# Sixteen of 98 target tiles of a graph propagation step summed from gathered feature rows instead of a dense product

## The reference

```python
def step(f, _):
    f = f * src_norm[:, None]
    agg = jax.ops.segment_sum(f[src], dst, num_segments=n)   # n = 12500 nodes, 200000 edges
    f = agg * dst_norm[:, None]
    f = (1.0 - ALPHA) * f + ALPHA * feat0
    return (f, None)
feat, _ = jax.lax.scan(step, feat, None, length=K)           # K = 10
x = x + feat
```

## Time and profile before

| | |
|---|---|
| median of three runs | 6389.11 us |
| span of the profiled execution | 7018.8 us |
| TensorE busy with matmuls in it | 5576.3 us (79%) |
| VectorE busy | 4279.1 us (61%) |
| GpSimd busy | 1693.3 us (24%) |
| mean granted TensorE clock | 0.880 |
| propagation: first to last sweep matmul | 3003 to 6987 us of the span |

### The profile page before, as it was taken

How to read it: one execution, slowest core, us unless ns; L and a number is a source line. 1 busy time by engine, 2 the same in 40 slices (tenths; PEclk the granted TensorE clock), 3 DMA queues, 4 the chain that set the end, 5 groups by cost and what they waited for, 6 DMA issues and landing times. The chain is left out here.

```text
span 7018.8 us, 211605 instructions
## 1 busy us (share of the span) xinstructions
PE 5576.3 (79%) x85008; PEld 3590.0 (51%) x85008; DVE 4279.1 (61%) x12668; ACT 721.3 (10%) x1695; POOL 1693.3 (24%) x1739
## 2 busy tenths in 40 slices
PE   1455555555555556589999999999999999999998
PEld 1344444444444445446565554656555565656564
DVE  7455555555555557766666666666656666666665
ACT  0122222222222223000000000000000000000000
POOL 5655555555555552500000000000000000000000
PEclk9867676666667767799999999999999999999999
DMA  4322222222222222155545555555555555555554
GB/s 117 77 75 76 76 76 77 75 76 77 79 72 79 72 76 94 27 205 194 200 183 204 192 198 205 189 200 191 201 191 201 191 201 201 189 203 189 197 197 169
DMA packets 442864, 1016.61 MB, mean 145 GB/s; under 512 B 253162, under 2 KB 371914, under 8 KB 387354
## 3 DMA queue, kind: packets, MB, share of 16 engines
q1 hardware_dynamic: 386938, 968.76, 39.0%
q0 software_dynamic: 54944, 33.96, 2.6%
HBM read 838.78 MB, written 176.58 MB: 145 GB/s over the span
## 5 line engine op out<-in xcount | busy, mean ns | idle before, releaser
L1864 PE MATMUL banks_fast<-count_units_fast,feature_parts_fast 128*32 128x512 fp8e3 x70608 | 3826.3, 379 | 31.6 <-DVE count_units_fast L1759 26.9
L1864 PEld LDWEIGHTS banks_fast<-count_units_fast,feature_parts_fast 128*32 128x32 bf16 x70608 | 2146.2, 97 | 1688.5 <-issue 37.5
L1758 DVE TENSOR_SCALAR count_units_fast<-packed_ring_fast 128x512 int32<-128x512 int32 x2949 | 1255.8, 426 | 1429.1 <-PE banks_fast L1864 1398.2
L144 POOL DMA_INDIRECT rows_fast<-row_table,idx_fast x1456 | 1408.5, 967 | 996.9 <-ACT count_stage_fast L1257 563.4
L1759 DVE TENSOR_SCALAR count_units_fast<-packed_ring_fast 128x512 int32<-128x512 int32 x2949 | 1237.2, 420 | 0.0
L1351 PE MATMUL banks_fast<-w1a_b1a_fast,turn_fast 49*128 49x96 f32 x3136 | 374.6, 375 | 810.6 <-ACT turn_fast L1262 589.6
L1223 DVE TENSOR_SCALAR window_place_hot_fast<-iota_wide_fast,local_keys_fast,target_weight_fast 128x196 bf16<-128x196 f16 x3136 | 933.9, 343 | 0.0
L1316 PE MATMUL banks_fast<-window_place_hot_fast,window_src_hot_fast 128*128 128x196 bf16 x3136 | 697.4, 312 | 115.4 <-issue 71.0
L1322 PE MATMUL banks_fast<-window_place_hot_fast,window_src_hot_fast 128*128 128x196 bf16 x3136 | 680.2, 305 | 106.1 <-issue 105.4
L1351 PEld LDWEIGHTS banks_fast<-w1a_b1a_fast,turn_fast 49*128 49x128 f32 x3136 | 294.9, 260 | 917.4 <-issue 497.4
L1316 PEld LDWEIGHTS banks_fast<-window_place_hot_fast,window_src_hot_fast 128*128 128x128 bf16 x3136 | 410.1, 155 | 224.2 <-issue 148.3
(11 more groups left out here) (282 smaller groups left out, 1551.5 us busy)
## 6 DMA issues: line engine op xcount, KB each, us to landing
packed_ring_fast<-edge_counts SPq DMA_DIRECT2D x422, 1792.0 KB, 7.0
edge_counts<-count_stage_fast SPq DMA_DIRECT2D x100, 784.0 KB
running_sums<-run_sums_fast SPq DMA_DIRECT2D x100, 768.0 KB
rows_fast<-row_table,idx_fast POOLq DMA_INDIRECT x1456
rows_fast<-attrs_padded SPq DMA_DIRECT2D x98, 128.0 KB
attrs_padded<-in_edge_attr SPq DMA_DIRECT2D x1, 12500.0 KB
rows_fast<-row_table,src_ends_fast POOLq DMA_INDIRECT x112
row_table<-h_nodes_fast SPq DMA_DIRECT2D x1, 1568.0 KB, 5.2
```

The source lines that it names most:

```text
L144: pool.indirect_dma_start(out=self.rows[:, r, c, 0:DN], out_offset=None, in_=b.dram.table, in_offset=bass.IndirectOffsetOnAxis(ap=idx[:, c ...
L1758: nc.vector.tensor_scalar(to[..., 0:P // 8], of, NIBBLES, None, ALU.bitwise_and)
L1864: last = nc.tensor.matmul(b.banks[at:at + DN, SWEEP[m % 2], 0:COLS], parts[:, side, j, k * DN:(k + 1) * DN], of_strip.bitcast(FP8), start= ...
```

## The change

The six blocks become five. The last sixteen target tiles (82 to 97) get no dense product. Since edges are sorted by target, the last 32,768 edges hold all edges of these tiles. They are cut into 256 gathers of 128 edges. For each, GpSimd gathers with an indirect DMA the 192-byte feature rows of the 128 source nodes from a table in DRAM (`feature_rows`, one for odd and one for even steps), and TensorE multiplies them with a one-hot matrix (`gathered_hots`, made once) of 128 edges by 128 targets: 96 weight columns, up to 128 moving columns. The 128 targets are a window that moves by 8 from gather to gather. The sums of four tiles fill a PSUM bank, and two banks are used in turn; a window that crosses from one bank to the next takes two matmuls, which makes 301 matmuls a step, and four zero matmuls of 512 columns clear the banks.

The table is written from the parts by DMAs on ScalarE's queue, ten a step: one behind each block's features, the head's and the four banks'. GpSimd begins a step's gathers when all ten of the step before have landed, and may be 32 gathers ahead of TensorE (eight slots of four). TensorE takes eight gathers at a time, a visit, between two sweep units; the units are given by a formula (unit 23, then one visit each 7.3 units, 32 visits, the last after unit 243 of 245). Banks are folded six units after their last visit, the fourth beside the fifth block's fold. VectorE has four more sets of features, of four tiles each. `x` is saved to DRAM and its tile holds the gathered rows; it comes back in the last step. Ahead of the loop, once: the edges' ends are loaded and turned, and VectorE makes the one-hots in eight instructions of 4096 columns. If an edge lies outside its window, the flag for the general way is set.

```diff
-BLOCKS = J // TILES
+BLOCKS = J // TILES - 1
+FIRST_GATHERED = HEAD + BLOCKS * TILES
+GATHERS = 256
+BANK_TILES = 4
+GROUP = 4
+GSLOTS = 8
+PE_GROUPS = 2
+PER_TARGET = E // N
+def window_of(c):
+    centre = (N - P * FIRST_GATHERED) - ((GATHERS - c) * P - P // 2) // PER_TARGET
+    return min(max(centre - P // 2, 0), TILES * P - P)
...
+        visit_unit = lambda visit: (230 + 73 * visit - (54 if visit >= 18 else 0)) // 10
+        fold_unit = [visit_unit(v) + FOLD_BEHIND for v in bank_visit[:-1]]
+        feature_unit = [u + LEAD for u in fold_unit]
...
         def _(pool):
+            with pool.Fori(0, steps2) as tt:
+                for side in range(2):
+                    t = tt * 2 + side
+                    pool.wait_ge(table_stored[side], tt * (STORES * 16) + (STORES * 16 if side else 16))
+                    for g in range(STEP_GROUPS):
+                        pool.wait_ge(group_used, t * STEP_GROUPS + (g + 1))
+                        for i in range(GROUP):
+                            c = g * GROUP + i
+                            pool.indirect_dma_start(out=rows[:, g % GSLOTS, i, :], out_offset=None, in_=b.dram.feature_rows[side],
+                                                    in_offset=bass.IndirectOffsetOnAxis(ap=idx[:, c:c + 1], axis=0)).then_inc(rows_in[g % GSLOTS], 16)
...
         def _(act):
+            def keep_block(t, side, m):
+                act.wait_ge(fresh, t * BLOCKS + (m + BLOCKS + 1))
+                keep_rows(1 - side, slice(HEAD + m * TILES, HEAD + (m + 1) * TILES))
...
+                    drain_bank(t, 3)
+                    drain_block(t, side, 4)
+                    keep_bank(t, side, 3)
+                    keep_block(t, side, 4)
...
         def _(dve):
+            for c in range(0, GATHERS, PIECE):
+                nc.vector.tensor_tensor(hots[:, c:c + PIECE, :], b.iota16[:, :].unsqueeze(1).broadcast_to([P, PIECE, P]),
+                                        local16[:, c:c + PIECE].unsqueeze(2).broadcast_to([P, PIECE, P]), ALU.is_equal).then_inc(hots_made, 1)
...
+                        if m == BLOCKS - 1:
+                            bank_features(t, q, side, GBANKS - 1)
+                        block_features(t, q, side, m)
...
         def _(pe):
+            def gathered_sums(t, visit):
+                for g in range(visit * PE_GROUPS, (visit + 1) * PE_GROUPS):
+                    pe.wait_ge(rows_in[g % GSLOTS], t * (STEP_GROUPS // GSLOTS * GROUP * 16) + (g // GSLOTS + 1) * (GROUP * 16))
+                    for i in range(GROUP):
+                        c = g * GROUP + i
...
+                        for lo, hi in ((w, cut), (cut, w + P)):
+                            if lo < hi:
+                                last = nc.tensor.matmul(b.banks[0:WF, GATHER_BANK[k % 2], lo - k * BANK_COLS:hi - k * BANK_COLS],
+                                                        rows[:, g % GSLOTS, i, :], hots[:, c, lo - w:hi - w].bitcast(FP8),
+                                                        start=False, stop=False, skip_group_check=True)
+                    last.then_inc(group_used, 1)
...
+            def sweep_and_gather(t, m, side, first, last_unit):
+                for v in range(first, last_unit):
+                    sweep_units(t, m, side, v, v + 1)
+                    at = m * BLOCK_UNITS + v
+                    for visit in range(GATHERS // per_visit):
+                        if visit_unit(visit) == at:
+                            gathered_sums(t, visit)
+                    if at in fold_unit:
+                        fold_bank(t, fold_unit.index(at))
...
+            pe.wait_ge(hots_made, GATHERS // 32)
             with nc.Fori(0, steps2, engines=[pe.engine], hint_back_edge=True) as tt:
...
-                        sweep_units(t, m, side, AHEAD, BLOCK_UNITS)
+                        sweep_and_gather(t, m, side, AHEAD, BLOCK_UNITS)
...
+                            fold_bank(t, GBANKS - 1)
-                        fold(t * BLOCKS + m, m % 2)
+                        fold(t * BLOCKS + m, half_of(side, m))
```

More of the change, by code:

```diff
@@ L87, in __init__ @@
         self.counts = dram("edge_counts", (CHUNKS, P, J + SLOTS, KC, P // 2), U8)
+        self.feature_rows = [dram(f"feature_rows{side}", (NP, WF), BF16) for side in range(2)]
+        self.x_saved = dram("x_saved", (P, J * DN))
 class Kept:
@@ L1734, in _ @@
+            act.dma_start(b.dram.x_saved, b.x[:, :]).then_inc(x_kept, 16)
+            keep_rows(0, slice(0, J))
             act.sem_inc(drained, 2)
             act.sem_inc(head_drained, 1)
-            with act.Fori(0, STEPS) as t:
-                for m in range(BLOCKS):
-                    n = t * BLOCKS + m
-                    act.wait_ge(unit_used, n * BLOCK_UNITS + (BLOCK_UNITS + UNITS))
-                    act.wait_ge(folded, n + 1)
-                    nc.scalar.copy(drain[:, m % 2, :], b.banks[:, SWEEP[m % 2], 0:COLS]).then_inc(drained, 1)
-                    if m == HEAD_AFTER:
-                        drain_head(t)
+            act.sem_inc(bank_drained, 2)
@@ L1790, in new_features @@
                 step(nc.vector.tensor_tensor(t1, per_node(got), spread(gain), ALU.mult))
-                dve.sem_inc(head_read if of_head else folds_read, 1)
+                dve.sem_inc(taken, 1)
                 step(nc.vector.scalar_tensor_tensor(out=f, in0=h, scalar=ALPHA, in1=t1, op0=ALU.mult, op1=ALU.add))
@@ L1800, in new_features, with block_features @@
                 assert steps[0] == CHAIN
-                dve.sem_inc(head_fresh if of_head else fresh, 1)
-            early = UNITS + AHEAD
-            open_units(0, 0, 0, early)
+                dve.sem_inc(done, 1)
+            def block_features(t, q, side, m):
+                dve.wait_ge(folded, t * BLOCKS + (m + 3))
+                new_features(q, side, b.banks[:, FOLD[half_of(side, m)], 0:TILES * DN], folds_read, fresh,
+                             slice(HEAD + m * TILES, HEAD + (m + 1) * TILES))
@@ L1805, in _ @@
+            make(nc.vector.tensor_tensor(unsorted[:, :], unsorted[:, :], bad(0), ALU.max))
+            for v in range(UNITS, early):
+                open_unit(0, 0, v)
+            dve.wait_ge(hots_made, GATHERS // PIECE)
             with dve.Fori(0, steps2) as tt:
@@ L1880, in sweep_head @@
                 last.then_inc(head_swept, 1)
+            def sweep_and_gather(t, m, side, first, last_unit):
[7 more added lines that the diff above has]
+                        fold_bank(t, fold_unit.index(at))
+            pe.wait_ge(ends_made, 3 + 8)
+            for of, what in enumerate((row_f, local_f)):
+                for h in range(2):
+                    at = of * GATHERS + h * P
+                    last = nc.tensor.transpose(b.banks[:, GATHER_BANK[0], at:at + P], what[:, h * P:(h + 1) * P], b.ident[:, :])
+            last.then_inc(ends_turned, 1)
             pe.wait_ge(stacked, STRIPS + 1)
```

257 lines of the change are left out of this document (209 added, 48 removed).

## The result

The kernel after took 6092.96 us (median of four runs, 6090.69 to 6094.23), the kernel before 6389.8 on the same chip: ratio 0.9538, 95% interval 0.9524 to 0.9551, or 297 us less. The forecast was 6304 with a range of 6190 to 6480: the sign was right, the gain over three times what was forecast, and the time outside the range.

The account below looks back on a forecast made before the run. TensorE alone was taken to bound each propagation step, falling from 398.1 to 384.3 us. Ten steps save 138 us, setup adds 47 and the tail 6: 6389 - 138 + 47 + 6 = 6304 us, range 6190 to 6480.

Parts of the forecast that it names:

- 32 visits that break the strips: TensorE, each propagation step: each visit stalls weight loads like a fold, 0.62 us, so 19.8 us a step.
- 301 gathered matmuls of 96 weight columns: TensorE, each step: load-heavy matmuls at 0.083 us each, 25.0 us a step (16.6 to 33.4).
- The sum of the step before: Old step on TensorE: 294 units 380.6, six folds 9.1, head 8.5, together 398.1 us, matching the measured step.
- the lower bound, 0.42: TensorE visits: the stall alone, 0.42 us each, giving 13.4 us a step.
- the fp32 loads of the head fold: Head fold on TensorE: load-bound fp32 loads 0.111 us apart, by columns 0.083 for 96 weight columns.
- the bf16 pairs: Matmuls of 128 weight and 196 moving columns, 0.087 us apart; lower bound 0.055 for 128 columns if loads hide.
- rival 1: Gathered matmuls on TensorE: loads hide, 0.055 us each, 8.4 us a step more saved, 6220 us; chance 0.18.
- its cheapest corner, 6156: TensorE visits: loads hide at 0.055 us a matmul and the stall is only 0.42 us, giving 6156 us.
- the limit of 1.42: GpSimd, each step: a gather may take (381.6 - 18) / 256 = 1.42 us before TensorE waits.
- Setup and tail: Before the loop: one-hots 35 us, loads 11, 47 in all; at the end: uncovered bank fold, features and store, 6.
- the rival price: One-hot setup on VectorE: eight instructions priced like all-bf16 ones, 2.7 us each, 20 us instead of 35.
- The 629.7 us: Profiled span's excess over the unprofiled median (7018.8 against 6389.11): claimed to lie wholly before the propagation.

Follow-up runs that it names:

- doubled matmuls: Kernel after with every gathered matmul issued twice: 6229.43 us, ratio 0.9762 to the kernel before.
- the run with 8 moving columns: Kernel after with an added matmul of 96 weight and 8 moving columns ahead of each gathered one: 6189.99 us, ratio 0.9698 to the kernel before.
- alternating pair: Kernel after with an added matmul of 32 weight and 8 moving columns ahead of each gathered one of 96: 6602.54 us, ratio 1.0347 to the kernel before.
- the kernel in strips: Kernel after with each gathered matmul of 96 weight columns cut into three of 32, same sums: 6053.48 us, ratio 0.9484 to the kernel before.

## Why the prediction was wrong, step by step

The step that failed is "32 visits that break the strips. Each stalls like a fold: 0.42 us, and 0.20 more", and beside it "301 gathered matmuls of 96 weight columns ... I take 0.083". Both are terms of the sum that were mis-sized, by 12.1 and 9.1 us of the 22 by which the step is shorter than forecast. Each was taken from the wrong cause: a visit pays for two changes of the weights' width, not for the stall of the loads, and a gathered matmul pays for its columns while its load hides. That TensorE bounds the step, and GpSimd only just does not, was as forecast.

| per step, us | forecast | measured | from |
|---|---|---|---|
| 245 units | 317.2 | 317.2 | openings 1.295 apart |
| visits' fixed part | 32 x 0.62 = 19.8 | 32 x 0.24 = 7.7 | doubled matmuls, strips |
| 301 matmuls | 25.0 | 15.9 | 211 at 0.056, 90 narrower at 0.045 |
| zero matmuls | 0.9 | 0.9 | a visit with one moves the openings by 0.91, not 0.69 |
| five block folds | 7.5 | 6.1 | openings move by 1.21 each |
| bank folds | 5.4 | 4.3 | 1.12 each, the one beside a block's 0.9 |
| head, and the loop's restart | 8.5 | 10.3 | 398.2 less 294 units and six folds of 1.21 |
| sum | 384.3 | 362.4 | without gathers: 362.3 |
| waits for rows | 0 | 1.3 | the step with gathers, 363.6, less that without |

- **The fixed part** was read off the break in the weight loads of a fold. In those rows the loads stand still and restart over 1.51 us, but the openings move by only 1.21: from the one at 3404.20 to the one below, eight units on and past VectorE's catching up, it is 11.57 us, less 8 x 1.295. The sum of the step before closed to 0.1 us all the same, since the rest was too small by as much as the folds were too large. In the first trace of before the openings give the head and its fold 9.5 us instead of 8.5, and where the loop over two steps begins again they move by 1.4 to 1.7, some 0.8 a step, for which the sum had no term. A closed sum proves its total, not its terms. Copied into 32 visits, the error had nothing to cancel it. Even the lower bound, 0.42, was the loads' idle time and not a bound on cost. The row, from the first trace of before:

```profile
3415.77 0.43 DVE L1758 TENSOR_SCALAR count_units_fast<-packed_ring_fast 128x512 int32<-128x512 int32 x1 [0.39 <-PE banks_fast L1864]
```

- **The matmul's 0.083** went by the fp32 loads of the head fold. The lower neighbour, the bf16 pairs, was the right one: 0.055 in the forecast (0.057 by its own 0.087 for 196 columns), 0.056 measured. The Trainium skill ("TensorE: Matmul & The Clock Gate") speaks of 128 weights as the condition for fast loading ("Weight-path perf modes") and gives a load columns over 1.2 ns ("LDWEIGHTS"), by which 96 columns would take an estimated 80 ns. The run with 8 moving columns has 0.045 for such a load and its matmul, so here the measurement differs, and it decides.
- **The forecast's rival 1** had the right mechanism for the matmuls (hidden loads), at 18 in 100; its cheapest corner, 6156, still paid 0.42 a visit. With 0.24 and its own 0.055 the prediction's sum gives 364 for a step and a time near 6100. The range ended at 6190 because it "leaves out ... the cheapest visits".
- **GpSimd**: forecast 1.30 us a gather, one a unit; measured 1.32 on average from start to start, median 1.295. Right, and so was that TensorE does not wait for it much. But the limit of 1.42 belonged to a step of 384. In one of 363.6 the same working gives (363.6 - 2.6 - 18) / 256 = 1.34, which leaves 6 us a step at the measured 1.316; eight more gathers found 5.7. (No row shows the 3 us for landing in that 18.) A limit that hangs on the step's length has to be worked out for each rival's step. The Trainium skill ("SBUF — State Buffer", "SBUF: two separate sides") has VectorE, in some kinds of instruction, hold a shared port pair for a whole instruction. The trace agrees for the one-hots (a gather of 4.36 us beside one of 4.41). Beside the unit openings gathers pay little: 0.99 us in the median of the propagation against 0.94 undisturbed.
- **Setup and tail**: 47 and 6 forecast. Setup 43.7, in it 34.8 for the one-hots (forecast 35; in the rival price, 8 x 2.7 is 22 and not 20); the tail 4.5 (from the start of the last sweep matmul to the end 36.6 instead of 32.1). Right.
- **The 629.7 us** ahead of the propagation: right.

## What to carry to other kernels

Price an interruption by how far it moves a steady rhythm across it (here the unit openings), not by the idle time that one queue shows in it: that queue runs ahead, and part of its gap is covered. Where a closed sum is used to price something new, check each reused term by itself, since two wrong terms can cancel. Matmuls that are slipped in between others are cheapest in the same weight shape: cut to the sweep's 32 columns, a visit here cost its columns and nothing more, though the step gave back only 2.9 of 7.7 us.

## What the runs showed of the hardware

- A change between weights of 32 and 96 columns costs about 0.1 us each time: 0.24 for a visit's two, 0.19 for the two of an alternating pair (0.21 less 0.022). Both widths alone are cheap: 0.022 and 0.045 us for a matmul of 8 moving columns. Weights of 32 columns here always fill one strip of the array and those of 96 three; no run separates which of the two, width or strips, makes the cost.
- A gather can be held through several VectorE instructions that stand back to back: one took 34.11 us beside the eight one-hots. That does not go for all instructions. In the kernel with one-hots between openings, gathers took 1.09 us beside openings that follow each other without a gap (the last three lines of its timeline above), and in the earlier trace rows one ended 0.12 us after an instruction, though the next had begun. What makes the difference was not tested.
- In the kernel in strips TensorE waits 4.3 to 5.2 us for nothing visible where its loop over two steps begins again (1.1 to 1.7 in the kernel after), and the granted clock falls behind it. Stretches of it around that point (busy us and instructions by engine, then granted clock, DMA share and GB/s):

```profile
3131.00:3139.00 8.00, 3.87 (x52) 2.96 (x43) 5.92 (x17) 0.01 (x1) 0.00 (x0) 1.00 0.64 243
3139.00:3142.70 3.70, 3.56 (x36) 1.68 (x40) 2.60 (x5) 0.00 (x0) 0.00 (x0) 0.54 0.02 5
3142.80:3160.00 17.20, 17.20 (x324) 9.52 (x320) 10.28 (x28) 0.00 (x0) 10.01 (x10) 1.00 0.53 169
```

For 3.7 us the granted clock is near the 1.2 GHz level. The loop body of this kernel holds 1,220 more matmuls than that of the kernel after, 14,330 against 13,110. Their number is not the reason: the kernel before has 14,804 in its own and idles 1.0 to 1.6 us there. The cause stays open. TensorE's first matmuls behind that idle time, in strips and then before:

```profile
3139.14 30.36 PE L2105 MATMUL banks_fast<-count_units_fast,feature_parts_fast 128*32 128x512 fp8e3 x528 [4.27 <-issue]
```
```profile
3808.08 7.30 PE L1864 MATMUL banks_fast<-count_units_fast,feature_parts_fast 128*32 128x512 fp8e3 x130 [1.33 <-issue]
```
